# Block-diagonal B built on VectorE and stores issued in another order, in a four-layer kernel with two selective scans

## The chip, the cores and the metric

The kernel runs as one program on one core of a Trainium2 chip. The metric is the device time of one execution in microseconds (us), the median of several executions. A core has five engines with queues of their own: PE (TensorE, matrix products; its weight loads are listed as PEld), DVE (VectorE), ACT (ScalarE), POOL (GpSimd) and SP, which here only issues DMA transfers. Engines wait for each other and for transfers through counting semaphores that the program sets.

## The reference

Input x is 4 x 1024 x 512 in float32. Four layers follow each other: full attention with a softmax, attention that is linear in the sequence length, and two state-space layers ("layer 2" and "layer 3" here, as in the names of the code). Layer 3 works on a permutation of the rows. The core of a state-space layer is

```
xz = xn @ W_in ; x_in, z = split(xz)             # 1024 channels each
u = silu(causal_conv4(x_in) + conv_b)
dt_r, B, C = split(u @ W_xp)                     # 64, 16, 16 wide
dt = softplus(dt_r @ W_dt + b_dt)
h = h * exp(dt[t] * A) + (dt[t] * u[t]) * B[t]   # 1024 channels x 16 states, along 1024 steps
y[t] = sum over states of h * C[t]
out = x + gate * (((y + u * D) * silu(z)) @ W_out)
```

## The kernel before

The program is a row of stages, each a block that all engines enter together, with its own tiles in on-chip memory (SBUF and PSUM); results go from stage to stage through scratch tensors in device memory. The stages are `project` p0 (normalisation and the q, k, v products), `attention`, `project` p1 (output product of the first layer), `linear_layer`, then `ssm_inputs` and `scan` for layer 2 and again for layer 3, and a final gather.

**project** loops over the 4 batch elements. Rows of a batch element arrive in one of two x buffers (`Rows.load`, two transfers of 1024 KB), DVE takes their statistics (`take_stats`, L387) when it reaches output o = 0 of the element before, and centres them (L410) after o = 2; PE turns them around between later outputs. SP issues everything in one order: the rows of element it + 1 at the start of element it (from it = 1 on), for p1 the residual rows, and then the store of each output tile. p0 has 24 outputs to an element, p1 has 8.

**ssm_inputs** also loops over the 4 elements, with one x buffer. For each there is a part in which x_in, the convolution (L1660, L1664) and u are made in 8 blocks m, and a part in which z, dt and the product dt*u are made in 8 blocks. dt*u is then turned by PE (`turn`, L1473) into PSUM, copied as a high part by ACT (`copy_hi`, L1550) and as a low part by DVE (`take_lo`, L1642) into a tile dT, of which there are two, and stored (`store_dT`, two transfers of 512 KB). The turns of element it are made between the x products of element it + 1: `copy_hi(it, m)` writes the tile that block m - 2 used, so it waits for that store to land. `turn` of block m waits for the low part of block m - 1. DVE, between `take_lo` and `convolve`, also takes the statistics of the rows of the next element, one block for each m. SP stores blocks m = 0 to 7 of an element's dT during the next element, one ahead of each uD store. For the last element, blocks 0 to 3 are turned and stored between the dt blocks and blocks 4 to 7 after the last four z outputs (`z_end`).

**scan** takes half sequences of 512 steps in 16 blocks per element, each with 16 states. PE makes the input term ("drive") as a product of dT with a block-diagonal matrix of B, `Bd`, 128 x (16, 32, 16): on partition p only the entries with t = p mod 32 are nonzero. ACT copies the drive from PSUM into h (`lay`, L2078) and makes the decays exp(dt*A) (`decay`, L2102); DVE runs the recurrence (L2171), POOL multiplies by C (L1938), PE adds over states (L1972). There are two `Bd` tiles, for the first and the second half of a sequence. At the start of the stage DVE clears both (L2176), then SP and ACT each issue 16 transfers of 4 KB that put the diagonal of the first one in place (L1805, L2090). The second one and all later contents are loaded during the scan in 32 transfers each, onto the places that stay the same.

The lines that start the scan on ACT are

```
            for n in range(4):
                lay(n)
            for k in range(LOOP):
                if k < UNITS_ALL:
                    decay(k)
                if k + 4 < UNITS_ALL:
                    lay(k + 4)
```

Of the kernel before, what the change touches and what calls it, by code (L numbers as in the profile page):

```python
# [13 lines left out]
F32R = mybir.dt.float32r  # L14
# [438 lines left out]
def project(core, name, ident, eps, io, cols, src, tab, func, jobs, scr=None):  # L453
# [4 lines left out]
    with ExitStack() as ctx:  # L458
# [174 lines left out]
        def _(sp):  # L633
# [13 lines left out]
            for it in range(B):  # L647
                if it >= 1 and it + 1 < B:
                    rows.load(sp, it + 1)
                if has_res:  # L650
                    for k in range(8):
                        if it >= 1:
                            sp.wait_ge(staged[k].handle, staged[k].at(it * uses))
                        sp.dma_start(res[k][:], jobs[0]["residual"][it, k * P:(k + 1) * P, :]
                                     ).then_inc(core.slot_in[k].handle, 16)
                for o, (n, a, b) in enumerate(outs):
                    slot, u, job = o % 8, it * uses + o // 8, jobs[n]
                    sp.wait_ge(staged[slot].handle, staged[slot].at(u + 1))
                    if job["kind"] == "T" and split:
                        tile = parts[slot][:].rearrange("p (s t) -> p s t", s=2)  # L660
                        dst = job["dst"][it, :, a * P:(a + 1) * P, b * HALF:(b + 1) * HALF].rearrange("s p t -> p s t")
                    elif job["kind"] == "T":
                        tile, dst = stage[slot][:], job["dst"][it, :, a, b * HALF:(b + 1) * HALF]
                    else:
                        tile, dst = value_of(slot), job["dst"][it, b * P:(b + 1) * P, a * D:(a + 1) * D]
                    sp.dma_start(dst, tile).then_inc(stored[slot].handle, 16)
                    if beside is not None and 1 <= it <= 2 and o == 4:
                        beside.load(sp, it)
                    if beside is not None and it == 3 and o == 12:
                        beside.store(sp)  # L670
# [637 lines left out]
def ssm_inputs(core, ident, cols, eps, io, scr, layer, src, tab, gather=None):  # L1308
# [5 lines left out]
    with ExitStack() as ctx:  # L1314
# [55 lines left out]
        def _(sp):  # L1370
# [26 lines left out]
            for it in range(B):  # L1397
                if gather is None and it + 1 < B:
                    rows.load(sp, it + 1)
                for m in range(IB + 1):  # L1400
                    if it and m < IB:
                        store_dT(it - 1, m)
                    if m >= 1:
                        w(sp, "uD", it * IB + m)
                        sp.dma_start(scr["uD"][it, m - 1], uD[(m - 1) % 2][:]).then_inc(uD_out[(m - 1) % 2].handle, 16)
# [10 lines left out]
                for m in range(IB):  # L1416
                    zs = {0: [z_with(it, k) for k in range(4)], 2: z_mid(it), 4: [z_with(it, k) for k in range(4, 8)]}.get(m, ())
                    for n in zs:
                        store_z(it, 2 * IB + n)
                        if it == B - 1 and m == 4:  # L1420
                            store_dT(it, zs.index(n))
                    w(sp, "dt", it * IB + (m + 1))
                    sp.dma_start(scr["dt"][it, m], dt[m % 4][:]).then_inc(dt_out[m % 4].handle, 16)
            for n in z_end(B - 1):
                store_z(B - 1, 2 * IB + n)
            for m in range(4, IB):
                store_dT(B - 1, m)
            for k in range(2):
# [112 lines left out]
        def _(act):  # L1541
# [19 lines left out]
            for it in range(B):  # L1561
# [39 lines left out]
                for group in (range(0, 4), range(4, 8)):  # L1601
# [27 lines left out]
                    for m in group:  # L1629
                        nc.scalar.activation(ea[m % 4][:], ea[m % 4][:], ACT.Ln, bias=eps[:, 2:3]).then_inc(c["log"].handle, 1)  # L1630
                for n in z_end(it):
                    take_z(n)
            for m in range(4, IB):
                copy_hi(B - 1, m)

        @block.vector
        def _(dve):
# [31 lines left out]
            for it in range(B):  # L1669
# [51 lines left out]
                if it + 1 < B:  # L1721
                    take_lo(it, 1)
                finish_dt(6)
                finish_dt(7)
            for m in range(4, IB):
                take_lo(B - 1, m)

# [18 lines left out]
def scan(core, ident, zero_eps, io, scr, layer, residual, dst):  # L1746
# [7 lines left out]
    with ExitStack() as ctx:  # L1754
# [22 lines left out]
        s.update({"o_" + n: core.count("out_" + n) for n in ("turned", "copied", "made", "gated")})  # L1777
        s.update({"last_" + n: core.count("last_" + n) for n in ("turned", "copied")})
        crep_in = core.slot_in[0:4]
        bd_in, dt_in, dT_in = core.input_in[0:2], core.input_in[2:4], core.slot_in[4:6]  # L1780
# [20 lines left out]
        def _(sp):  # L1801
            def load_B(half, rows):
                b, th = half // 2, half % 2
                for t in rows:
                    sp.dma_start(Bd[th][t::TC, :, t, :],  # L1805
                                 scr["Bcol"][b, th, :, t].rearrange("j c (k n) -> j (c k) n", n=NS)).then_inc(bd_in[th].handle, 16)
# [65 lines left out]
            def store_o(n):  # L1872
                w(sp, "o_gated", n + 1)
                sp.dma_start(dst[n // TT, n % TT * P:(n % TT + 1) * P, :], o[:]).then_inc(o_out.handle, 16)

            sp.dma_start(A[:], scr["A"][layer - 2].rearrange("i p e -> p i e")).then_inc(s["A_in"].handle, 16)
            load_dt(0)
            load_dT(0)
            load_C(0, 0)
            w(sp, "cleared", 1)  # L1880
            load_B(0, range(0, TC, 2))
            for q in range(1, 4):
                load_C(0, q)
            load_dT(1)
            load_dt(1)
            w(sp, "cleared", 2)
            for blk in range(BLOCKS + IB + 2):
# [57 lines left out]
        def _(pe):  # L1945
            def make_drive(n):
# [5 lines left out]
                if n % 8 == 0:  # L1952
                    pe.wait_ge(dT_in[j].handle, dT_in[j].at(64 * (blk // 2 + 1)))
                    if m == 0:
                        pe.wait_ge(bd_in[th].handle, bd_in[th].at(16 * TC * (b + 1)))
                if n >= 1:
# [114 lines left out]
        def _(act):  # L2071
# [15 lines left out]

            w(act, "cleared", 1)
            for t in range(1, TC, 2):
                act.dma_start(Bd[0][t::TC, :, t, :],  # L2090
                              scr["Bcol"][0, 0, :, t].rearrange("j c (k n) -> j (c k) n", n=NS)).then_inc(bd_in[0].handle, 16)
            act.wait_ge(s["A_in"].handle, s["A_in"].at(16))
# [19 lines left out]
            def copy_late(step):  # L2112
# [6 lines left out]
                nc.scalar.copy(dst_, src_).then_inc(s["last_copied"].handle, 1)  # L2119

            for n in range(4):
                lay(n)
            for k in range(LOOP):
                if k < UNITS_ALL:
                    decay(k)
# [13 lines left out]
        def _(dve):  # L2139
# [61 lines left out]
    s["carried"].stage_added(UNITS_ALL // 8)  # L2201
    s["cleared"].stage_added(2)
    s["A_in"].stage_added(16)
    for k in range(2):
        bd_in[k].stage_added(16 * TC * B)
        dt_in[k].stage_added(16 * BLOCKS // 2)
# [152 lines left out]
```

## Time and profile before

| | us |
|---|---|
| median of 3 runs | 6346.13 (6344.94 to 6351.1) |
| the profiled execution | 6348.06 |
| its span, first to last instruction | 6346.3 |
| busy PE, DVE, ACT, POOL | 5510.1, 4684.1, 4206.4, 2482.3 |
| first instruction of scan 2, of scan 3 | 2922.56, 4947.09 |

The profile is one execution. Times of rows are microseconds from the start of the span, unless they are marked ns. A row of the timeline merges like instructions of one engine that follow each other: start, length of the stretch, engine, line, operation, output and inputs, how often; in brackets how long the engine had been idle before and who released it. SPq and ACTq rows are DMA issues; their length is the time of issuing. PEclk is the granted TensorE clock as a share of full speed.

### The profile page before, as it was taken

The page shows a single profiled execution, that of the slowest core. Times are in us where ns is not written, and L with a number is a line of the kernel's source. Part 1 is how long each engine was busy: PE and PEld are TensorE (multiplying, and loading weights), DVE is VectorE, ACT ScalarE, POOL GpSimd, SP SyncE. Part 2 cuts the span into 40 slices and gives each one's busy share as a digit, 9 for nine tenths or more (in the row PEclk, how much of TensorE's full clock was granted, in tenths as well). Part 3 has the DMA queues.
Part 4 walks back from the last instruction along what each step waited for, and adds up shares of the span by engine and source line. Part 5 has one row for each costly group of instructions (what it writes and reads, how often), then busy time and mean ns, then how long its engine had stood idle before and what let it go on. Part 6 is the DMA issues. An engine that isn't in the chain of part 4 may idle for free. (4 is left out here: it accounts for less than half of the span.)

```text
span 6346.3 us, 85966 instructions
## 1 busy us (share of the span) xinstructions
PE 5510.1 (87%) x30568; PEld 3517.3 (55%) x30568; DVE 4684.1 (74%) x5708; ACT 4206.4 (66%) x6218; POOL 2482.3 (39%) x1098
## 2 busy tenths in 40 slices
PE   8989999997899989995788888879999578888884
PEld 3456666664455534444666666654444466666662
DVE  3359999995545445546999999964555799999993
ACT  2148888883232235556989999954555799999981
POOL 0000000000000000003999999960000699999994
PEclk9999999998999999997999999999999899999997
DMA  6463333413211133336556566632444555665554
GB/s 232 183 150 68 87 78 81 101 35 144 102 44 50 34 115 147 148 135 190 151 153 162 161 162 160 158 110 90 148 150 155 171 152 160 156 159 156 158 144 175
DMA packets 571129, 842.72 MB, mean 133 GB/s; under 512 B 100544, under 2 KB 239936, under 8 KB 570704
## 3 DMA queue, kind: packets, MB, share of 16 engines
q1 hardware_dynamic: 559248, 811.92, 43.7%
q0 software_dynamic: 5120, 16.78, 0.8%
q10 hardware_dynamic: 6336, 8.52, 0.4%
q8 instruction: 246, 4.03, 0.3%
q14 instruction: 179, 1.47, 0.1%
HBM read 544.23 MB, written 292.81 MB: 132 GB/s over the span
## 5 line engine op out<-in xcount | busy, mean ns | idle before, releaser
L1938 POOL TENSOR_TENSOR scan_hC<-scan_h,scan_Crep 128x1024 f32<-128x1024 f32 x1024 | 2395.8, 2374 | 2413.8 <-DVE scan_h L2171 2392.9
L2102 ACT ACTIVATE scan_a<-scan_dt,scan_A 128x512 f32<-128x512 f32 x2048 | 1368.4, 697 | 91.0 <-DVE scan_h L2171 73.9
L1972 PE MATMUL scan_y<-ident,scan_hC 128*128 128x128 f32 x8192 | 1113.2, 279 | 293.9 <-POOL scan_hC L1938 288.3
L1972 PEld LDWEIGHTS scan_y<-ident,scan_hC 128*128 128x128 f32 x8192 | 903.8, 141 | 681.5 <-POOL scan_hC L1938 631.3
L2171 DVE TENSOR_TENSOR_SCAN scan_h<-scan_a,scan_carry,scan_h 128x512 f32<-128x512 f32 x1024 | 1216.6, 1258 | 17.0 <-ACT scan_a L2102 14.0
L2171 DVE TENSOR_TENSOR_SCAN scan_h<-scan_a,scan_h 128x512 f32<-128x512 f32 x1024 | 1155.0, 1198 | 59.3 <-ACT scan_a L2102 58.7
L2078 ACT COPY scan_h<-scan_drive 128x1024 f32<-128x1024 f32 x1024 | 1042.1, 1018 | 168.4 <-PE scan_drive L1960 156.4
L1960 PE MATMUL scan_drive<-scan_Bd,scan_dT 128*128 128x256 f32 x4096 | 750.3, 305 | 127.5 <-ACT scan_h L2078 76.5
L1960 PEld LDWEIGHTS scan_drive<-scan_Bd,scan_dT 128*128 128x128 f32 x4096 | 558.1, 192 | 180.6 <-issue 93.8
L861 DVE CUSTOM_DVE_ANT_0 att_sm<-att_S,att_mneg 128x1024 f32<-128x1024 f32 x512 | 621.8, 1215 | 16.5 <-POOL att_mneg L787 16.2
L919 ACT ACTIVATE att_pr<-att_sm,att_nmax 128x1024 f32<-128x1024 f32 x512 | 590.6, 1154 | 58.0 <-DVE att_nmax L861 45.5
L811 PE MATMUL att_TP<-ident,att_pr 128*128 128x128 f32 x4096 | 548.4, 277 | 12.6 <-ACT att_pT L904 12.6
L811 PEld LDWEIGHTS att_TP<-ident,att_pr 128*128 128x128 f32 x4096 | 457.3, 141 | 136.5 <-issue 52.0
L1492 PE MATMUL ssmin_ring<-ssmin_Wz,ssmin_xT 128*128 128x512 f32 x1024 | 462.1, 602 | 8.2 <-ACT ssmin_zt L1567 8.2
L1998 PE MATMUL scan_O<-scan_Wo,scan_gT 128*128 128x512 f32 x896 | 456.9, 593 | 0.0
L1492 PE MATMUL ssmin_ring<-ssmin_xT,ssmin_Wx 128*128 128x512 f32 x1024 | 454.6, 599 | 0.0
L869 DVE COPY att_pT<-att_TP 128x512 f32<-128x512 f32 x512 | 352.6, 689 | 100.1 <-PE att_TP L811 100.1
L787 POOL TENSOR_SCALAR att_mneg<-att_mrow 128x1024 f32<-128x1024 f32 x4 | 14.6, 3639 | 1011.4 <-DMA att_mrow<-mask 753.2
L800 PE MATMUL att_S<-att_k,att_q 128*128 128x512 f32 x1024 | 370.9, 444 | 18.7 <-DMA att_k<-scratch_k_split 11.5
L1684 DVE TENSOR_SCALAR ssmin_dt<-ssmin_DTP,column_tables 128x1024 f32<-128x1024 f32 x64 | 82.2, 1284 | 410.7 <-PE ssmin_DTP L1525 410.7
L904 ACT COPY att_pT<-att_TP 128x512 f32<-128x512 f32 x512 | 295.0, 576 | 105.4 <-PE att_TP L811 105.4
L1492 PEld LDWEIGHTS ssmin_ring<-ssmin_Wz,ssmin_xT 128*128 128x128 f32 x1024 | 190.4, 191 | 259.3 <-issue 236.7
(188 smaller groups left out, 6173.5 us busy)
## 6 DMA issues: line engine op xcount, KB each, us to landing
scan_dT<-scratch_dtuT SPq DMA_DIRECT2D x512, 256.0 KB, 6.1
scratch_dtuT<-ssmin_dT SPq DMA_DIRECT2D x128, 512.0 KB, 3.6
scan_Crep<-scratch_bc SPq DMA_DIRECT2D x64, 1024.0 KB, 9.5
att_q<-scratch_q_split SPq DMA_DIRECT2D x256, 128.0 KB, 4.5
att_k<-scratch_k_split SPq DMA_DIRECT2D x256, 128.0 KB, 4.7
scratch_uD<-ssmin_uD SPq DMA_DIRECT2D x64, 512.0 KB, 3.4
scratch_z<-ssmin_zt SPq DMA_DIRECT2D x128, 256.0 KB, 2.2
scratch_dt<-ssmin_dt SPq DMA_DIRECT2D x64, 512.0 KB, 2.6
```

Source lines behind the costliest of these rows:

```text
L800: last = nc.tensor.matmul(S[u % 2][:, half * HALF:(half + 1) * HALF], q[slot][:, t * P:(t + 1) * P].bitcast(F32R), k[slot][:, half * HALF: ...
L811: last = nc.tensor.transpose(TP[:, m * P:(m + 1) * P], pr[u % 2][:, m * P:(m + 1) * P], ident[:])
L861: nc.vector.tensor_tensor_reduce(sm[u % 2][:], S[u % 2][:], mneg[b % 2][:], -1.0, HUGE, ALU.add, ALU.min, nmax[u % 2][:]).then_inc(s["shif ...
L919: nc.scalar.activation(pr[u % 2][:], sm[u % 2][:], ACT.Exp, bias=nmax[u % 2][:, 0:1], scale=-1.0, accum_out=psums[:, u // PAIRS % 4, j, se ...
L1492: last = nc.tensor.matmul(ring[e % 4][:], lhs, rhs, start=(kt == 0), stop=(kt == KT - 1))
L1938: nc.gpsimd.tensor_tensor(hC[k % 2][:], of, Crep[:, 2 * p:2 * p + 2, :], ALU.mult).then_inc(s["scaled"].handle, 1)
L1960: last = nc.tensor.matmul(drive[:, c * TC:(c + 1) * TC, :], dT[j][:, at * P:(at + 1) * P].bitcast(F32R), Bd[th][:, at, :, first:first + GS ...
L1972: last = nc.tensor.matmul(y[j][:, t, :], hC[k % 2][:, i, t * P:(t + 1) * P], ident[:], start=(p == 0 and i == 0 and t == 0), stop=False, i ...
L1998: last = nc.tensor.matmul(O[:], gT[:, m, :], Wo[:, m, :], start=(m == 0), stop=(m == IB - 1))
L2078: nc.scalar.copy(h[group % 3][:, :, tt * P:(tt + 1) * P], drive[:].rearrange("p t n -> p n t")).then_inc(s["laid"].handle, 1)
L2102: nc.scalar.activation(a[(2 * k + i) % 3][:], dt[j][:], ACT.Exp, scale=A[:, m, 2 * p + i:2 * p + i + 1]).then_inc(s["decayed"].handle, 1)
L2171: nc.vector.tensor_tensor_scan(of, a[(2 * k + i) % 3][:], of, first, ALU.mult, ALU.add).then_inc(s["scanned"].handle, 1)
```

## The change

The first `Bd` of a scan is no longer cleared and filled by 32 small transfers. SP loads B as plain columns, 128 x 256 values, with one transfer (`raw`, in the tile o that is free then). DVE makes a mask (`diag`: 1 where t = p mod 32) by two small additions from the identity, and writes `Bd[0]` by 8 multiplications of 128 x 1024 (`spread`), each a quarter of the chunks and half of the states; PE's first 8 drives wait for one of them each. Then DVE clears `Bd[1]` as before. ACT issues no transfers and makes the first decays ahead of its first four copies. SP's three later C loads, dT(1) and dt(1) no longer wait for a cleared `Bd`.

In `ssm_inputs` the stores of dT blocks 0 and 1 move from the next element's first part to just ahead of the dt stores of blocks 4 and 6; the rows of element it + 2 (layer 2 only) are loaded ahead of the store of dt block 6 instead of at the start of element it + 1; and at the end of the last element the four z outputs, the four `copy_hi`, the four `take_lo` and their stores are interleaved. In `project` the rows of element it + 2 are loaded after the store of output o = 1 of element it.

```diff
-                if it >= 1 and it + 1 < B:
-                    rows.load(sp, it + 1)
...
                     sp.dma_start(dst, tile).then_inc(stored[slot].handle, 16)
+                    if o == 1 and it + 2 < B:
+                        rows.load(sp, it + 2)
...
-                if gather is None and it + 1 < B:
-                    rows.load(sp, it + 1)
+                if gather is None and it == 0:
+                    rows.load(sp, 1)
                 for m in range(IB + 1):
-                    if it and m < IB:
+                    if it and 2 <= m < IB:
                         store_dT(it - 1, m)
...
+                    if it + 1 < B and m in (4, 6):
+                        store_dT(it, m // 2 - 2)
+                    if gather is None and it + 2 < B and m == 6:
+                        rows.load(sp, it + 2)
+                    if it == B - 1 and m >= 6:
+                        store_z(it, 2 * IB + z_end(it)[m - 6])
+                        if m == 7:
+                            store_dT(it, 4)
                     w(sp, "dt", it * IB + (m + 1))
                     sp.dma_start(scr["dt"][it, m], dt[m % 4][:]).then_inc(dt_out[m % 4].handle, 16)
-            for n in z_end(B - 1):
-                store_z(B - 1, 2 * IB + n)
-            for m in range(4, IB):
-                store_dT(B - 1, m)
+            store_z(B - 1, 2 * IB + z_end(B - 1)[2])
+            store_dT(B - 1, 5)
+            store_z(B - 1, 2 * IB + z_end(B - 1)[3])
+            store_dT(B - 1, 6)
+            store_dT(B - 1, 7)
...
-                for n in z_end(it):
+                for n, m in zip(z_end(it), range(4, IB)):
                     take_z(n)
-            for m in range(4, IB):
-                copy_hi(B - 1, m)
+                    copy_hi(it, m)
...
                 finish_dt(5)
                 if it + 1 < B:
                     take_lo(it, 1)
+                else:
+                    take_lo(it, 4)
                 finish_dt(6)
+                if it == B - 1:
+                    take_lo(it, 5)
                 finish_dt(7)
-            for m in range(4, IB):
-                take_lo(B - 1, m)
+            take_lo(B - 1, 6)
+            take_lo(B - 1, 7)
...
+            sp.dma_start(raw, scr["Bcol"][0, 0].rearrange("j t c e -> (j t) (c e)")).then_inc(raw_in.handle, 16)
             sp.dma_start(A[:], scr["A"][layer - 2].rearrange("i p e -> p i e")).then_inc(s["A_in"].handle, 16)
             load_dt(0)
             load_dT(0)
             load_C(0, 0)
-            w(sp, "cleared", 1)
-            load_B(0, range(0, TC, 2))
             for q in range(1, 4):
                 load_C(0, q)
             load_dT(1)
             load_dt(1)
-            w(sp, "cleared", 2)
...
+                if n < SPREAD:
+                    w(pe, "cleared", n + 1)
...
-            w(act, "cleared", 1)
-            for t in range(1, TC, 2):
-                act.dma_start(Bd[0][t::TC, :, t, :],
-                              scr["Bcol"][0, 0, :, t].rearrange("j c (k n) -> j (c k) n", n=NS)).then_inc(bd_in[0].handle, 16)
...
+            decay(0)
             for n in range(4):
                 lay(n)
             for k in range(LOOP):
-                if k < UNITS_ALL:
+                if 1 <= k < UNITS_ALL:
                     decay(k)
...
-            for k in range(2):
-                zeros = zero_eps[:, 1:2].broadcast_to([P, NC * TC * NS])
-                nc.vector.tensor_copy(Bd[k][:].rearrange("p c t n -> p (c t n)").bitcast(F32R), zeros
-                                      ).then_inc(s["cleared"].handle, 1)
+            def spread(n):
+                tt, first = n % 4, n // 4 * GS
+                values = raw.rearrange("p (a o n) -> p a o n", o=1, n=NS)[:, tt::4, :, first:first + GS]
+                places = diag.rearrange("p (o t q) -> p o t q", o=1, q=1)
+                shape = [P, NC // 4, TC, GS]
+                nc.vector.tensor_tensor(Bd[0][:, tt::4, :, first:first + GS].bitcast(F32R), values.broadcast_to(shape),
+                                        places.broadcast_to(shape), ALU.mult).then_inc(s["cleared"].handle, 1)
...
+            for n in range(SPREAD):
+                spread(n)
+            zeros = zero_eps[:, 1:2].broadcast_to([P, NC * TC * NS])
+            nc.vector.tensor_copy(Bd[1][:].rearrange("p c t n -> p (c t n)").bitcast(F32R), zeros
+                                  ).then_inc(s["cleared"].handle, 1)
```

## Rows read from the trace of the kernel before

**Rows 1.** Scan 2: stretch, busy PE, PEld, DVE, ACT, POOL, clock, DMA, GB/s.

```profile
3000.00:3100.00 100.00, 69.39 (x537) 60.77 (x538) 99.76 (x93) 95.83 (x141) 100.00 (x44) 1.00 0.53 143
```

**Rows 2.** Timeline, the start of scan 2.

```profile
2922.56 0.36 SPq L1876 DMA_DIRECT2D scan_A<-scratch_A  x1
2922.59 8.76 DVE L2176 CAST scan_Bd<-eps 128x8192 fp32r<-128x8192 f32 x2 [4.66 <-PEq L1314]
...
2923.59 1.85 SPq L1822 DMA_DIRECT2D scan_dT<-scratch_dtuT  x4
...
2927.05 13.07 SPq L1805 DMA_DIRECT2D scan_Bd<-scratch_Bcol  x16
...
2941.58 1.20 PE L1960 MATMUL scan_drive<-scan_Bd,scan_dT 128*128 128x256 f32 x4 [24.99 <-DMA scan_Bd<-scratch_Bcol]
...
2950.88 1.28 ACT L2102 ACT_TABLE_LOAD   x1
...
2952.97 9.13 DVE L2171 TENSOR_TENSOR_SCAN scan_h<-scan_a,scan_h 128x512 f32<-128x512 f32 x8 [21.61 <-ACT scan_a L2102]
```

**Rows 3.** DMA rate in 40 slices of 0.35 us from 2923; issues, size, us to landing.

```profile
GB/s 0 12 107 98 140 293 304 345 228 211 199 170 217 228 217 199 258 199 199 187 199 205 164 228 228 322 386 374 393 383 211 72 34 35 31 30 20 24 20 14
...
scan_dt<-scratch_dt SPq DMA_DIRECT2D x1, 256.0 KB, 4.5
scan_A<-scratch_A SPq DMA_DIRECT2D x1, 68.0 KB, 2.2
```

**Rows 4.** Instructions by line and shape: count, busy us, mean ns, idle before.

```profile
L1693 DVE TENSOR_TENSOR ssmin_u<-ssmin_dt,ssmin_u 128x1024 f32<-128x1024 f32 x64 | 78.4, 1225 | 2.2
...
L1204 DVE TENSOR_TENSOR lin_q<-lin_q,lin_qmax 128x2048 f32<-128x2048 f32 x8 | 18.3, 2292 | 0.3
...
L1697 DVE TENSOR_TENSOR ssmin_BT<-ssmin_X,ssmin_BT 128x128 fp32r<-128x128 f32 x8 | 2.3, 292 | 10.7 <-ACT ssmin_BT L1619 10.7
```

**Rows 5.** Timeline, the end of layer 2's inputs; page, one line of the issues.

```profile
2903.82 4.67 SPq L1375 DMA_DIRECT2D scratch_z<-ssmin_zt  x4
2906.86 1.28 ACT L1567 ACTIVATE ssmin_zt<-ssmin_ring 128x512 f32<-128x512 f32 x2 [6.43 <-DMA scratch_z<-ssmin_zt]
...
2914.66 0.69 DVE L1642 TENSOR_TENSOR ssmin_dT<-ssmin_X,ssmin_dT 128x512 fp32r<-128x512 f32 x1 [0.16 <-ACT ssmin_dT L1550]
...
2917.24 0.69 DVE L1642 TENSOR_TENSOR ssmin_dT<-ssmin_X,ssmin_dT 128x512 fp32r<-128x512 f32 x1 [0.16 <-ACT ssmin_dT L1550]
...
scratch_dtuT<-ssmin_dT SPq DMA_DIRECT2D x128, 512.0 KB, 3.6
```

**Rows 6.** Timeline by engine, layer 2's inputs, from element 0 to 1.

```profile
2445.57 2.04 PE L1473 MATMUL ssmin_X<-ident,ssmin_u 128*128 128x128 f32 x8 [7.40 <-DVE ssmin_dT L1642]
...
2443.88 0.59 ACT L1550 CAST ssmin_dT<-ssmin_X 128x512 fp32r<-128x512 f32 x1 [12.82 <-DMA scratch_dtuT<-ssmin_dT]
...
2438.93 0.69 DVE L387 BATCH_NORM_STATS2 ssmin_st<-ssmin_x 128x6 f32<-128x512 f32 x1 [5.13 <-DMA ssmin_x<-scratch_x]
...
2444.76 0.67 DVE L1642 TENSOR_TENSOR ssmin_dT<-ssmin_X,ssmin_dT 128x512 fp32r<-128x512 f32 x1
...
2432.93 1.40 SPq L379 DMA_DIRECT2D ssmin_x<-scratch_x  x2
```

**Rows 7.** Timeline by engine, p1, from element 0 on.

```profile
1550.35 1.94 PE L420 MATMUL p_bank<-ident,p_x 128*128 128x128 f32 x8 [5.74 <-DVE p_x L410]
...
1565.62 17.33 PE L542 MATMUL p_bank<-p_W,p_xT 128*128 128x512 f32 x40
1588.61 1.94 PE L420 MATMUL p_bank<-ident,p_x 128*128 128x128 f32 x8 [5.66 <-DVE p_x L410]
...
1538.56 2.47 DVE L387 BATCH_NORM_STATS2 p_st<-p_x 128x6 f32<-128x512 f32 x4 [6.23 <-DMA p_x<-scratch_y]
```

**Rows 8.** Busy us by engine (columns as in rows 1), p0 from element 0 to 1.

```profile
120.00:140.00 20.00, 20.00 (x95) 7.58 (x94) 11.23 (x27) 5.62 (x8) 0.00 (x0) 1.00 0.44 160
```

**Rows 9.** Timeline, DVE's first recurrence of scan 3.

```profile
4978.11 9.13 DVE L2171 TENSOR_TENSOR_SCAN scan_h<-scan_a,scan_h 128x512 f32<-128x512 f32 x8 [22.22 <-ACT scan_a L2102]
```

More of the change, by code:

```diff
@@ L1778, in scan @@
         s.update({"last_" + n: core.count("last_" + n) for n in ("turned", "copied")})
+        raw_in = core.stage_stored[6]
+        raw, diag, pairs = o[:, 0:NC * NS], o[:, NC * NS:NC * NS + TC], o[:, NC * NS + TC:NC * NS + 3 * TC]
+        SPREAD = 8
         crep_in = core.slot_in[0:4]
@@ L1803, in load_B @@
                 b, th = half // 2, half % 2
+                if half == 1:
+                    w(sp, "cleared", SPREAD + 1)
                 for t in rows:
@@ L1953, in make_drive @@
                     pe.wait_ge(dT_in[j].handle, dT_in[j].at(64 * (blk // 2 + 1)))
-                    if m == 0:
-                        pe.wait_ge(bd_in[th].handle, bd_in[th].at(16 * TC * (b + 1)))
+                    if m == 0 and b + th >= 1:
+                        pe.wait_ge(bd_in[th].handle, bd_in[th].at(16 * TC * (b + th)))
+                if n < SPREAD:
+                    w(pe, "cleared", n + 1)
                 if n >= 1:
@@ L2172, in recur @@
                                                  ).then_inc(s["scanned"].handle, 1)
-            for k in range(2):
-                zeros = zero_eps[:, 1:2].broadcast_to([P, NC * TC * NS])
-                nc.vector.tensor_copy(Bd[k][:].rearrange("p c t n -> p (c t n)").bitcast(F32R), zeros
-                                      ).then_inc(s["cleared"].handle, 1)
+            def spread(n):
[5 more added lines that the diff above has]
+                                        places.broadcast_to(shape), ALU.mult).then_inc(s["cleared"].handle, 1)
+            nc.vector.tensor_tensor(pairs, ident[:, 0:2 * TC], ident[:, 2 * TC:4 * TC], ALU.add
+                                    ).then_inc(core.scalar_step.handle, 1)
+            dve.wait_ge(core.scalar_step.handle, core.scalar_step.at(1))
+            nc.vector.tensor_tensor(diag, pairs[:, 0:TC], pairs[:, TC:2 * TC], ALU.add
+                                    ).then_inc(core.scalar_step.handle, 1)
+            dve.wait_ge(core.scalar_step.handle, core.scalar_step.at(2))
+            dve.wait_ge(raw_in.handle, raw_in.at(16))
+            for n in range(SPREAD):
[3 more added lines that the diff above has]
+                                  ).then_inc(s["cleared"].handle, 1)
             for k in range(LOOP):
@@ L2201, in scan @@
     s["carried"].stage_added(UNITS_ALL // 8)
-    s["cleared"].stage_added(2)
+    s["cleared"].stage_added(SPREAD + 1)
+    core.scalar_step.stage_added(2)
+    raw_in.stage_added(16)
     s["A_in"].stage_added(16)
     for k in range(2):
-        bd_in[k].stage_added(16 * TC * B)
+        bd_in[k].stage_added(16 * TC * (B - 1 + k))
         dt_in[k].stage_added(16 * BLOCKS // 2)
```

## The prediction

> **What bounds the kernel now.** I read the page's slices first, then busy time by stage, then the timeline of each place that the diff touches, with the list of waits beside it to see which releaser comes last. No engine bounds the whole. In a scan it is DVE: in 100 us of scan 2 it is busy 99.76 [rows 1]. POOL and ACT are almost full there too, but their work follows DVE's. So a scan ends as much earlier as its first recurrence begins, as long as ACT and the dT loads keep up. In p0 PE never pauses, the border between two elements included [rows 8]. In p1 and in the first part of an element of `ssm_inputs` PE runs without a pause but for a hole at each border [rows 6, 7]. Thus three kinds of place can give something: the start of each scan, the end of each input stage (the next stage starts after it), and the holes at borders.
>
> **Start of a scan.** I count from T0, SP's first issue (2922.56). Now: DVE clears 2 x 4.4, the small transfers begin at T0+4.5 and hold PE until T0+19.0, four drives and lays take until T0+28.3, then a table load, the first decay, and the recurrence starts at T0+30.4 [rows 2]. In scan 3 DVE has idled 22.22 instead of 21.61, so it is T0+31.0 [rows 2, 9].
>
> After the change two paths run side by side.
>
> DVE: `raw` is 128 KB. The nearest rows are A, 68 KB in 2.2, and dt, 256 KB behind it, in 4.5 [rows 3]. It is first in the queue; I take 2.6, bounds 2.2 and 4.5. The two small additions end before that. The 8 spreads write 1024 elements each; a product of that size of two full operands takes 1.225, and one of 2048 with a repeated operand 2.292, so repeating costs nothing [rows 4]. Writing and reading in short runs: a low part of 128 elements in runs of 16 takes 0.292 [rows 4], which leaves no room for a large price per run, but runs of 8 with a repeated middle dimension are not in the trace. I take 1.15 from start to start (half of 2.292), 9.2 for eight; bounds 1.1 (the same rows less overlap) and 2.34 (128 elements in 0.292 scaled to 1024). The clear of `Bd[1]` adds 4.4. DVE is free at T0+2.6+9.2+4.4 = T0+16.2, bounds T0+15.4 and T0+27.6.
>
> The VectorE page speaks against a product here. The Trainium skill ("VectorE: DVE Perf Modes", "Why `tensor_tensor` can't do 2×_2P or 4×") has a float32 product of two tensors at one element per cycle where a copy makes two. The trace agrees: 1.20 ns an element against 0.53, the cleared `Bd` [rows 2, 4]. At the page's 0.96 GHz eight spreads would be 8.5, and DVE free 0.7 sooner, which by the next paragraph changes nothing.
>
> PE and ACT: the first drive now needs the first spread (T0+3.8) and dT(0). dT(0) is 4 x 256 KB, issued from T0+1.0 to T0+2.9 [rows 2]. From 2925.8 on the queues move about 210 GB/s, before the small transfers of B have begun [rows 3], so this is the rate of dT's own short rows; adding the slices, the 1.38 MB of A, dt and dT(0) are through at 2930.6, T0+8.0. `raw` ahead adds 0.4, and completion about 0.5. I take T0+8.8, bounds T0+7.0 (at the 345 of the best slice before) and T0+10.5. From the first drive to the end of the fourth lay it is 9.3 [rows 2]; the table load and the first decay lie in the wait before. The recurrence starts at T0+18.2: dT(0) decides, and the spreads have 2 us of slack. The second decay now stands behind lay 4 (a drive and lay take 2.3), where it was ready before; I take 0.5 for DVE's pause there. Gain: 30.4 - 18.2 - 0.5 = 11.7 in scan 2, 31.0 - 18.7 = 12.3 in scan 3, **24.0** in all; bounds for the two 6 (slow spreads: T0+27.6) and 29 (T0+16.2, where DVE decides).
>
> [...]
>
> SP is now free at once for 3 MB of C, dT(1) and dt(1). C's four parts and dT(1) follow dT(0): 4.2 MB at the 380 of the full slices, then 1.05 MB at 210, ends near T0+25.5; the ninth drive wants dT(1) near T0+27. Slack 1.5, so nothing; it is the first thing to be late.
>
> **End of an input stage.** Now z output 14 waits 6.43 for the store of z 12, which SP issues only behind four dt stores (2903.82), and all four copies of dT stand behind it; the last low part ends at 2917.93 [rows 5]. Afterwards `copy_hi(4)` runs at once behind z 12 (about 2900), and low part 4 is done at 2901.8. Blocks 5 to 7 each need `finish_dt` of the block (2.4) and the chain of turn, high and low part (2.58 from one block's last low part to the next's) [rows 4, 5]. Written out: low part 5 ends 2905.5, finish 7 ends 2907.9, low part 6 about 2909.4; `copy_hi(7)` needs the store of block 5, issued at 2907.5 behind dt 7 and z 14 and landing in 3.6 [rows 5], 2911.5, and the last low part ends about 2913.2. The 4.6 until the next stage stay. Gain 4.7 a stage, **9.4** for two; bounds 3 (store landing 5) and 6 (no store waited for) each.
>
> **p1.** DVE waits 6.23 for rows that SP loads only at the border, and PE 5.74 and 5.66 for the centred rows [rows 7]. An element's PE work is 64 products at 17.33/40 and 4 turns of some 0.9, 31.2, and the turns are 38.26 apart: 7.1 lost per border, pause and slower clock behind it together (the first turn after it takes 1.94) [rows 7]. Afterwards the rows are issued over 15 us before they are wanted. DVE then does statistics 5.6 earlier than PE's fourth product ends, output 2, and centres half in 1.9: PE waits perhaps 0.2. The second border's slow stretch looked a little longer, so I take 7.7 each, **15.4** for two; bounds 12 and 16.5.
>
> **Borders in layer 2's inputs.** ACT waits 12.82 for the store of dT(0), but that wait is not worth 12.82. Low part 2 starts at 2444.76, just when DVE is through with waiting for x (5.13, until 2438.93), statistics and a convolution; the high part was there about then as well [rows 6]. With dT(0) stored early, x alone decides. Its issue moves from 2432.93 to about 2429.6, but behind 1 MB of dT(1) where it had 0.5 MB of dt: +0.9. I take 2.4 for each of two borders, **4.8**; bounds 0 and 3.3 each. From element 2 to 3 and in layer 3 SP loads no x and DVE is the last already: 0.
>
> **p0.** PE is full [rows 8]; the moved loads give nothing. In element 0 SP now stands after o = 1 until the turn of the rows (a few us) and 2 MB go ahead of later stores; the slots come up for reuse 27 us after, so 0.
>
> **Sum.** 24.0 + 9.4 + 15.4 + 4.8 = 53.6. Against the profiled 6348.06 (span 6346.3) that gives 6294.5; the median is 1.9 below the profiled one, so **6292.5**. A measurement tells about 0.2%, 12.7 us.
>
> **Rivals.**
>
> *The spreads are slow* (short runs at 2.34 each): DVE decides at T0+27.6, no pause behind. Gain 2.8 + 3.4 = 6.2 in place of 24.0: 6310. For: the only row of such short runs; against: its fixed part. 0.10.
>
> *dT(0) or dT(1) is the late one*: 5.3 MB crowd one queue where 1.4 MB stood; if dT(1) is 3 us late or dT(0) comes at T0+10.5, each scan loses 2 to 3: 6298. 0.15.
>
> *The early rows give nothing in p1*, because centring or the residual loads then hold PE: 6292.5 + 15.4 = 6308. Against: DVE has 20 us of work in 31. 0.05.
>
> *dT(0) is early*: at the best slice's 345 GB/s it is there at T0+7.0, the fourth lay ends about when DVE is free (T0+16.2), DVE decides, and the scans give 2 x 2 more less a pause of DVE: 6288.5. Against: dT's own slices at 210. 0.10. [...]
>
> *Slower*: the spreads decide so strongly that the scans start later than now. Place: DVE, T0. With 29.6 gained elsewhere, each scan must start 14.8 later than T0+30.7, thus 8 spreads over 38.5, 4.8 each, four times the row. At 6.5 each (5.3 times) DVE is free at T0+59, 28.3 later than now per scan: 6346.1 - 29.6 + 56.6 = 6373. No row is near it. 0.02.
>
> *The change doesn't do what it says*, same within 0.2%: stores and loads land as late as before, and the scans lose to contention what they gain. 0.03.
>
> The forecast itself, 6284 to 6301, has 0.55. The range that leaves out no more than 2 in 10 is 6280 to 6310. Faster by over 0.2%: 0.95; within: 0.03; slower: 0.02.
>
> **What the profile of the changed kernel would show.** The first recurrence 18 to 19 after SP's first issue, released by ACT (decay or lay), with DVE idle some 2 before it; spreads near 1.15; PE's first drive released by the dT transfer. PE's holes in p1 gone and its clock 1.0 there. ACT without the 12.8 wait at layer 2's borders, but PE's 7.4 only down to about 5, with DVE still waiting for x. From the first instruction after the last dt group to scan's start 4.7 less. The prediction is wrong if spreads take over 1.4, if DVE pauses in the first 40 us of a scan for laid or dT, or if ACT waits over 3 for a dT store at an input stage's end.

## The result, and the profile after it

The changed kernel takes 6303.5 us (median of four, 6299.29 to 6306.85) where the kernel before takes 6348.2 beside it: a ratio of 0.9927 with a 95% interval of 0.9912 to 0.9942, by which the gain is 46 (37 to 56). Run again later it was at 0.9944 (0.9928 to 0.9960), a gain of 36 (25 to 46). The forecast was 6292.5 with a range of 6280 to 6310, a gain of 53.6. So the sign and the range held, the time is 11 above the forecast, and the gain is 7 to 18 below it. The profiled execution took 6299.29, span 6297.5: 48.8 less span than before.

Where the span went, from the same marks in both traces (an issue or a first instruction of each stage). Each stretch is one execution against one, and the scans differ between executions by more than 10, as is shown further below.

| mark | before | after | gain up to it | gain of the stretch | forecast |
|---|---|---|---|---|---|
| last copy of attention's output | 1464.8 | 1465.6 | -0.8 | -0.8 | 0 |
| first turn of the linear layer | 1655.95 | 1640.84 | 15.1 | p1: 15.9 | 15.4 |
| rows issued for layer 2's inputs | 2240.80 | 2225.39 | 15.4 | 0.3 | 0 |
| first issue of scan 2 | 2922.56 | 2900.97 | 21.6 | inputs: 6.2 | 9.5 |
| index load of layer 3's inputs | 4267.3 | 4230.8 | 36.5 | scan 2: 14.9 | 11.7 |
| first issue of scan 3 | 4947.09 | 4908.49 | 38.6 | inputs: 2.1 | 4.7 |
| index load of the gather | 6263.9 | 6214.5 | 49.4 | scan 3: 10.8 | 12.3 |
| end | 6346.3 | 6297.5 | 48.8 | -0.6 | 0 |

**Start of a scan** (beside [rows 2]): timeline of the kernel after, scan 2.

```profile
2900.97 0.33 SPq L1893 DMA_DIRECT2D scan_o<-scratch_Bcol  x1
...
2902.44 1.85 SPq L1839 DMA_DIRECT2D scan_dT<-scratch_dtuT  x4
...
2903.05 9.17 DVE L2194 TENSOR_TENSOR scan_Bd<-scan_o 128x1024 fp32r<-128x1024 f32 x8 [1.60 <-DMA scan_o<-scratch_Bcol]
2912.14 4.42 DVE L2207 CAST scan_Bd<-eps 128x8192 fp32r<-128x8192 f32 x1
...
2910.76 1.22 PE L1977 MATMUL scan_drive<-scan_Bd,scan_dT 128*128 128x256 f32 x4 [18.86 <-DMA scan_dT<-scratch_dtuT]
2913.18 1.19 PE L1977 MATMUL scan_drive<-scan_Bd,scan_dT 128*128 128x256 f32 x4 [1.19 <-ACT scan_h L2095]
...
2905.84 1.28 ACT L2115 ACT_TABLE_LOAD   x1 [11.07 <-DMA scan_dt<-scratch_dt]
2907.13 1.30 ACT L2115 ACTIVATE scan_a<-scan_dt,scan_A 128x512 f32<-128x512 f32 x2
...
2919.18 1.01 ACT L2095 COPY scan_h<-scan_drive 128x1024 f32<-128x1024 f32 x1 [1.38 <-PE scan_drive L1977]
...
2920.23 2.34 DVE L2185 TENSOR_TENSOR_SCAN scan_h<-scan_a,scan_h 128x512 f32<-128x512 f32 x2 [3.67 <-ACT scan_h L2095]
2923.28 7.11 DVE L2185 TENSOR_TENSOR_SCAN scan_h<-scan_a,scan_h 128x512 f32<-128x512 f32 x6 [0.71 <-ACT scan_a L2115]
```

T0 is SP's first issue of the scan, here 2900.97. The first drive comes at T0+9.8, released by dT(0); DVE is through with the spreads and the clear at T0+15.6, waits 3.67 for the fourth lay, and the recurrence starts at T0+19.3. The last row has the pause that follows, 0.71, behind the second decay. By the slices under the next heading the 1.51 MB of `raw`, A, dt(0) and dT(0) are through at about T0+8.2 (an estimate, adding them up), and the first drive begins 1.6 after that. In scan 3 the recurrence starts at 4927.45, T0+19.0.

**dT(1).** DMA rate of the kernel after in 40 slices of 0.875 from 2900.

```profile
GB/s 0 0 155 133 222 262 206 206 225 213 199 213 384 382 391 386 384 391 386 386 389 386 384 346 183 208 213 222 201 204 267 211 0 0 173 295 187 227 211 174
```

C runs at 380 to 390, then dT(1), dt(1) and uD at some 210 to 2928. The ninth drive, the first on dT(1), begins at 2930.07 with no wait in front of it. dT(1) has a slack of 2 at least.

**p1** (beside [rows 7]): timeline of the kernel after.

```profile
1545.16 1.06 PE L420 MATMUL p_bank<-ident,p_x 128*128 128x128 f32 x8
...
1576.32 1.06 PE L420 MATMUL p_bank<-ident,p_x 128*128 128x128 f32 x8
...
1590.15 31.07 PE L542 MATMUL p_bank<-p_W,p_xT 128*128 128x512 f32 x72
...
1532.81 4.84 DVE L387 BATCH_NORM_STATS2 p_st<-p_x 128x6 f32<-128x512 f32 x8
```

No pause stands before a turn, and the turns are 31.16 apart, where 38.26 was. DVE takes the statistics of all eight blocks at one go.

**Border in layer 2's inputs** (beside [rows 6]): timeline of the kernel after, element 0 to 1.

```profile
2413.98 0.97 SPq L1381 DMA_DIRECT2D scratch_dtuT<-ssmin_dT  x2
2414.99 2.17 SPq L379 DMA_DIRECT2D ssmin_x<-scratch_x  x2
...
2422.18 0.69 DVE L387 BATCH_NORM_STATS2 ssmin_st<-ssmin_x 128x6 f32<-128x512 f32 x1 [2.84 <-DMA ssmin_x<-scratch_x]
...
2428.83 1.94 PE L1482 MATMUL ssmin_X<-ident,ssmin_u 128*128 128x128 f32 x8 [5.12 <-DVE ssmin_dT L1650]
```

ACT's wait of 12.82 for a dT store is gone: none of the 50 copies of high parts from 2400 to 2850 waits for a store. PE's hole went from 7.40 to 5.12 only, and DVE still waits for x.

**End of layer 2's inputs** (beside [rows 5]): timeline of the kernel after, last element.

```profile
2883.53 0.43 SPq L1375 DMA_DIRECT2D scratch_z<-ssmin_zt  x1
2884.01 1.52 SPq L1381 DMA_DIRECT2D scratch_dtuT<-ssmin_dT  x2
2886.76 0.33 SPq L1431 DMA_DIRECT2D scratch_dt<-ssmin_dt  x1
2887.14 1.07 SPq L1375 DMA_DIRECT2D scratch_z<-ssmin_zt  x1
2888.26 1.97 SPq L1381 DMA_DIRECT2D scratch_dtuT<-ssmin_dT  x2
...
2888.03 0.58 ACT L1559 CAST ssmin_dT<-ssmin_X 128x512 fp32r<-128x512 f32 x1 [4.19 <-DMA scratch_dtuT<-ssmin_dT]
...
2892.75 0.59 ACT L1559 CAST ssmin_dT<-ssmin_X 128x512 fp32r<-128x512 f32 x1 [2.24 <-DMA scratch_dtuT<-ssmin_dT]
...
2894.80 0.69 DVE L1650 TENSOR_TENSOR ssmin_dT<-ssmin_X,ssmin_dT 128x512 fp32r<-128x512 f32 x1 [0.73 <-ACT ssmin_dT L1559]
2901.00 0.22 DVE L2197 TENSOR_TENSOR scan_o<-ident 128x64 f32<-128x64 f32 x1 [5.51 <-PEq L1314]
```

From `finish_dt(4)`, DVE's first step that completes dt of block 4 (2875.29; 2895.02 before), to the end of the last low part it is 20.2 now and was 22.9. But from there to the scan's first issue it is 5.5, and was 4.6: the end gave 1.9. In layer 3 the same marks give 20.2 and 5.4, also 1.9. What SP waits for last in the stage is the landing of the last dT store (waits of SP, kernel before and after, at the end of layer 2's inputs):

```profile
SPq L1432 <- DMA scratch_dtuT<-ssmin_dT: 3.4, 1, 3.4
SPq L1441 <- DMA scratch_dtuT<-ssmin_dT: 3.8, 1, 3.8
```

SP's last issue ends 0.4 after the last low part before (2918.32) and 0.8 after it now (2896.30); the scan's first issue comes 4.2 and 4.7 behind that.

### The profile page after: what moved, and what is told of

The parts are those of the page before. It is cut to its first block and busy times, and to the rows that moved or that the text cites. A ratio compares the mean times of both kernels' runs of the same rounds, so it can differ in the third digit from the quotient of the medians.

```text
span 6297.5 us, 85938 instructions
## 1 busy us (share of the span) xinstructions
PE 5498.4 (87%) x30568; PEld 3509.0 (56%) x30568; DVE 4694.3 (75%) x5726; ACT 4204.3 (67%) x6218; POOL 2483.5 (39%) x1098
```

## The experiments

### The parts one by one

Four kernels are the kernel before with one part of the diff each, word for word as in the diff above: `project` alone, `ssm_inputs` alone, `scan` alone, and `ssm_inputs` without what it changes at the last element's end.

> The kernel before with the change in `project` alone (rows of element it + 2 loaded after output o = 1). By the prediction p1 gives 15.4 (bounds 12 to 16.5) and p0 nothing, so a ratio of 0.9976 to the kernel before; by the changed kernel's profile p1 gave 15.9 and p0 with attention lost 0.7, which would be a ratio of 0.9976 too if that loss is the change's own and 0.9975 if not. If the rows gave nothing the ratio is 1.000. In the profile PE has no pause over 1 us ahead of its turns in p1, and DVE's statistics don't wait for rows.

> The kernel before with the whole change in `ssm_inputs` alone. By the prediction 14.2 (two borders 4.8, two stage ends 9.4), a ratio of 0.9978. By the changed kernel's profile 8.3 (borders 4.3, ends 1.9 and 2.1), a ratio of 0.9987. If the difference between the two is other work that slid, and not the ends, this run comes out at the first of them.

> The kernel before with the whole change in `scan` alone. By the prediction 24.0 (each scan starts 12 us earlier), a ratio of 0.9962. By the changed kernel's profile the starts gave 21.4 net of DVE's pauses, and scan 2 ran another 3.8 faster in its later part at a clock of 1.00 where it had been 0.97 to 0.98: if that is the execution's and not the change's, the ratio is 0.9966; if the change brings it, 0.9960. First recurrence at 19.3 after SP's first issue in scan 2.

> The kernel before with the change in `ssm_inputs` but for the last element's end, which stays as before: only dT blocks 0 and 1 are stored earlier and the rows are loaded earlier. By the prediction 4.8, a ratio of 0.9992; by the changed kernel's profile 4.3. The run before this one less this one is what the two stage ends give: 9.4 by the prediction, 4.0 by the profile.

| kernel | ratio (95% interval) | gain |
|---|---|---|
| `project` | 0.9976 (0.9967 to 0.9985) | 15 (10 to 21) |
| `ssm_inputs` | 0.9980 (0.9972 to 0.9989) | 13 (7 to 18) |
| `scan` | 0.9984 (0.9975 to 0.9993) | 10 (4 to 16) |
| `ssm_inputs`, borders only | 0.9994 (0.9984 to 1.0005) | 4 (-3 to 10) |

`project` agrees with the 15.4 forecast, with 5 either way, and so do the borders as far as they can be told. The two ends can't be told from the difference of the second row and the last (9, with over 8 either way), only from the traces: from `finish_dt(4)` to layer 2's scan it is 25.7 in the profile of `ssm_inputs` alone and 27.5 in the one without the ends, which is the 1.9 again. `scan` is the surprise: its profile has the first recurrence at T0+19.2 and T0+20.5, but the time fell by 10 (4 to 16), not by 21 to 24.

### The scan's part in its place

Two kernels on one chip: the changed kernel again, and the changed kernel with the old `scan`.

> The changed kernel once more, on one chip with the three others of this group. 46 below the kernel before (ratio 0.9927, as at first). The three parts measured one by one gave 15.2, 12.7 and 10.2, together 38 (0.9940). If the scan's part was mis-measured or falls away when it stands alone, this run stays near 0.9927; if 0.9927 was a lucky one, it comes out near 0.9940.

> The changed kernel with the scan of before: project and inputs are changed, the scan isn't. By the parts measured alone 27.9 below the kernel before (0.9956). What the run before this one has over it is the scan's part in its real place: 21 to 24 by the starts of the scans in the profile (19.3 in place of 30.4, less 0.9 of pauses, twice), 10 by the run with the scan's change alone. In the latter case the later part of the scans is longer, and the DVE idle time by stretches of 100 us must show where.

The changed kernel came out at 0.9944 (0.9928 to 0.9960), five runs of mean 6307.4. With the old scan it was 0.9961 (0.9947 to 0.9976), five runs of mean 6320.8. The scan's part is 13 here, with runs of 6297.8 to 6317.9 against 6311.6 to 6325.2. The profiles with the same start sequence say where the rest went (the two scans together; "rest" is from the first recurrence to the end of the stage, scan 2 and scan 3):

| kernel | starts at T0+ | rest | both scans |
|---|---|---|---|
| before | 30.4, 31.0 | 1314.3, 1285.8 | 2661.5 |
| `project` alone | 29.9, 30.5 | 1303.8, 1283.8 | 2648.0 |
| `ssm_inputs` alone | 29.7, 30.3 | 1313.7, 1285.1 | 2658.8 |
| borders alone | 30.6, 30.8 | 1310.0, 1285.6 | 2657.1 |
| after, old scan | 30.5, 30.2 | 1319.0, 1281.4 | 2661.1 |
| after | 19.3, 19.0 | 1310.6, 1287.1 | 2635.8 |
| `scan` alone | 19.2, 20.5 | 1322.1, 1289.1 | 2650.9 |
| after, again | 19.2, 20.2 | 1313.9, 1285.2 | 2638.3 |
| after, rows earlier (below) | 19.4, 19.4 | 1313.2, 1287.2 | 2639.2 |
| after, stores earlier (below) | 19.0, 19.4 | 1321.5, 1286.6 | 2646.5 |

The starts are 10.9 earlier a scan on average (mean 30.4 of 29.7 to 31.0, and 19.4 of 19.0 to 20.5), 21.9 for two. The whole scans are 15.2 shorter on average (2657.3 and 2642.1). The rest of scan 2 differs by 15 between the executions of the old scan and by 12 between those of the new one, as much as the part to be measured. One stretch of the kernel with `scan` alone shows what such a difference is made of: busy us by engine, columns as in [rows 1].

```profile
3272.00:3277.00 5.00, 3.04 (x23) 2.21 (x21) 5.00 (x5) 3.73 (x7) 3.29 (x2) 1.00 1.04 334
3277.00:3282.00 5.00, 2.24 (x18) 1.83 (x16) 3.87 (x5) 4.14 (x6) 2.73 (x2) 1.00 1.06 242
3282.00:3287.00 5.00, 3.96 (x19) 3.96 (x20) 3.34 (x4) 1.34 (x4) 5.00 (x3) 0.53 0.71 161
3287.00:3292.00 5.00, 4.72 (x33) 4.48 (x31) 2.34 (x2) 3.46 (x7) 4.05 (x3) 0.79 0.59 170
3292.00:3297.00 5.00, 3.41 (x26) 2.72 (x25) 4.99 (x5) 5.00 (x8) 3.81 (x3) 1.00 1.00 250
```

PE is busy 5.3 of 10 us (3272 to 3282). Then the granted clock falls to 0.53 in a stretch of 5 us and is 0.79 in the next. DVE is busy 5.7 of these last 10 us where it is full otherwise. From 3276 to 3294 it waits 4.5 for decays, which stand in ACT's queue behind lays, and ACT waits 7.2 for PE's drives. The pause of PE that comes before has a source in the same trace, POOL's wait for a load of C:

```profile
3273.71 4.66 POOL L1941 TENSOR_TENSOR scan_hC<-scan_h,scan_Crep 128x1024 f32<-128x1024 f32 x2 [2.04 <-DMA scan_Crep<-scratch_bc]
3280.64 6.97 POOL L1941 TENSOR_TENSOR scan_hC<-scan_h,scan_Crep 128x1024 f32<-128x1024 f32 x3 [2.27 <-DMA scan_Crep<-scratch_bc]
```

PE then waits 1.96, 0.75 and 3.05 for POOL's products. In scan 2 POOL waits 3.4 to 15.4 for C in the fourteen profiles of this document. The four with over 10.5 are the four with the longest rest, 1319.0 to 1322.1; the ten others have 1303.8 to 1314.3. That ties the rest of scan 2 to the loads of C, but no run changed these loads, so that they cause the difference is not shown.

Stretches of 100 us with a clock under 1.00, beyond the first, number two to six in scan 2 and none to three in scan 3 of the ten profiles. In the mean over these profiles 6.7 are missing between 21.9 and 15.2. DVE idles 1.1 in the first 100 us of a scan where it idled 0.5, mostly the pause behind the second decay: 1.3 for two scans. In the eleven stretches of 100 us behind it it idles 31.5 in both scans where it idled 27.5, above all in those with a clock under 1.00: 4.0. The last 1.4 I can't place.

Whether the new scan itself brings more of this is not settled for scan 2. For scan 3 the table leans to yes, and the four other kernels with the new scan, described below, more so: their rest of scan 3 is 1290.8 (spreads twice), 1293.5 (dT(0) first), 1296.2 and 1289.6 (the two kernels of all together). Of nine executions with the new scan eight are above the longest of the five with the old one (1285.8). Some 0.6 a scan of this is the pause behind the second decay. What in the new scan brings the rest is open.

### Who decides the start

Three kernels change one thing in the changed one. The first makes every spread twice:

```diff
             for n in range(SPREAD):
-                spread(n)
+                for again in range(2):
+                    spread(n, again)
```

> The changed kernel with each of the 8 spreads made twice (the first one waited for, then the same again). It measures how much slack the spreads have. The prediction's theory is that dT(0) decides and DVE has slack: the profile after shows DVE free 15.6 after SP's first issue and the fourth lay's end at 19.2, a slack of 3.6. Eight more spreads are 9.2 to 10, so DVE is free at about 25 to 25.6, the first recurrence comes at about 25.5 in place of 19.3, and DVE's later pauses of 0.9 go: 5 to 5.5 a scan, 10 to 11 in all over the changed kernel (ratio to the kernel before 0.9943). If DVE decided, each scan would lose the full 9.2 to 10, 18 to 20 in all (0.9957).

The sixteen spreads took 19.25, DVE was free at T0+25.8, and the recurrences started at T0+25.7 and T0+25.6, with DVE idle before neither. So 10.1 more on DVE moved the start by 6.4: DVE had 3.7 of slack, as the wait for the fourth lay in the profile after says, and dT(0) with its four drives and lays decides. By time it was 0.9954 (0.9940 to 0.9968), 17 more than the first run of the changed kernel and 6 more than the second, around the 11 expected.

The second issues dT(0) earlier:

```diff
-            sp.dma_start(A[:], ...)
-            load_dt(0)
             load_dT(0)
+            sp.dma_start(A[:], ...)
+            load_dt(0)
```

> The changed kernel with the four transfers of dT(0) issued ahead of those of A and dt(0), right behind raw. If dT(0) decides, its 324 KB less in front bring it 1 us to 1.5 us earlier, and the first drive, the fourth lay and the first recurrence with it, as DVE is free 3.6 before: 2 to 3 in all over both scans (ratio 0.9923). dt(0) and A then land near 11.5, the first decay comes ahead of the first lay and holds it up by up to 1.5, which could eat the gain. If DVE decides, nothing.

Timeline of this kernel, scan 2 (T0 is 2903.99).

```profile
2911.78 1.22 PE L1977 MATMUL scan_drive<-scan_Bd,scan_dT 128*128 128x256 f32 x4 [16.82 <-DMA scan_dT<-scratch_dtuT]
...
2912.91 1.28 ACT L2115 ACT_TABLE_LOAD   x1 [15.10 <-DMA scan_dt<-scratch_dt]
2914.20 1.30 ACT L2115 ACTIVATE scan_a<-scan_dt,scan_A 128x512 f32<-128x512 f32 x2
...
2915.44 1.00 ACT L2095 COPY scan_h<-scan_drive 128x1024 f32<-128x1024 f32 x1
```

The first drive comes at T0+7.8, 2.0 earlier, and nothing is gained: the recurrence starts at T0+19.7. ACT's queue now has the first decay waiting for dt(0) in front of lay 0, and lay 0 comes at T0+11.4, where it came at T0+11.1. That is the wait behind a moved instruction that I had named as a risk. The time was 0.9933 (0.9916 to 0.9949), no difference from the changed kernel that can be told.

### Borders and ends

> The changed kernel with the rows of element it + 2 in layer 2's inputs loaded ahead of the store of dt block 5, not of block 6 behind the store of dT(1). By the prediction x alone decides at the border: DVE's wait of 2.84 for it goes, and PE's hole falls from 5.12 to about 2.3: 2.8 for each of two borders, 5.6 in all (ratio 0.9918). The rival is that ACT's wait for the store of dT(0) comes back, as that store now stands behind 1 MB: then less than 2 in all.

```diff
-                    if gather is None and it + 2 < B and m == 6:
+                    if gather is None and it + 2 < B and m == 5:
                         rows.load(sp, it + 2)
```

(the line also stands ahead of `store_dT` now). DVE's wait for x is gone, ACT waits for no dT store, and PE's hole is down to 2.18:

```profile
2430.58 1.71 PE L1482 MATMUL ssmin_X<-ident,ssmin_u 128*128 128x128 f32 x8 [2.18 <-DVE ssmin_dT L1650]
```

From the load of the first weight to the scan's load of A it is 665.8 where the changed kernel has 674.4 and 674.2. That is 8.5, more than the 5.6 expected; x did decide. The two holes account for 6.3 of it (5.12 and 5.54 fell to 2.18 each); the rest I did not follow up. The time was 0.9927 (0.9910 to 0.9943), which can't show it.

> The changed kernel with the stores of dT blocks 4 and 5 of the last element ahead of the dt stores of blocks 6 and 7. In the profile after, the store of block 4 is issued 2.0 after its low part is done, and ACT's high part 6 waits 4.19 for it; block 5's store is issued 2.6 after, and high part 7 waits 2.24. If the place in SP's order is what lost the ends, high part 7 and all behind it come 2 to 2.6 earlier in each of the two layers: 4 to 5 in all (ratio 0.9920). If the landing time decides and SP's order doesn't, under 1 in all.

```diff
                     if it == B - 1 and m >= 6:
                         store_z(it, 2 * IB + z_end(it)[m - 6])
-                        if m == 7:
-                            store_dT(it, 4)
+                        store_dT(it, m - 2)
...
-            store_dT(B - 1, 5)
```

Timeline of this kernel.

```profile
2885.87 0.58 ACT L1557 CAST ssmin_dT<-ssmin_X 128x512 fp32r<-128x512 f32 x1 [2.43 <-PE ssmin_X L1480]
...
2890.05 4.15 SPq L1381 DMA_DIRECT2D scratch_dtuT<-ssmin_dT  x4
...
2890.93 0.69 DVE L1648 TENSOR_TENSOR ssmin_dT<-ssmin_X,ssmin_dT 128x512 fp32r<-128x512 f32 x1 [0.16 <-ACT ssmin_dT L1557]
2898.91 0.23 DVE L2195 TENSOR_TENSOR scan_o<-ident 128x64 f32<-128x64 f32 x1 [7.29 <-PEq L1314]
```

No high part waits for a store any more, and from `finish_dt(4)` to the last low part it is 16.7, 3.5 less. But the stage's end then stands 7.3 behind the last low part, not 5.5. Half of what the chain gains is given back. The place is SP's queue: its stores now stand close together, the last four issues take 4.15, and the last of them ends 2.6 behind the last low part, where it was 0.8. From that issue to the scan's first it is 4.7, as in the changed kernel. The net is 1.7 in each layer by the traces, against the 2 to 2.6 expected. By time it was 0.9935 (0.9919 to 0.9952), no difference that can be told.

### All of it together

> The changed kernel with three things together: rows loaded ahead of dt block 5's store at layer 2's borders, dT blocks 4 and 5 stored ahead of dt 6 and 7 at the inputs' ends, and in the scan dT(0) issued behind raw, ahead of A and dt, with the first decay split around the first lays (lay 0, half, lay 1, half, lay 2, lay 3), so that it doesn't stand ahead of lay 0. Borders 2.9 each, 5.8; ends about 1.6 for layer 2 and 1 for layer 3; scans: first drive at T0+7.8, fourth lay done at about T0+17.7, first recurrence at T0+17.8 in place of 19.3, 1.5 each. 11 less than the changed kernel. If DVE decided the start instead, the scans give nothing and it is 8.

> The run before this one, and PE makes 32 transposes of the identity into the unused output bank at the start of each scan, while it waits for dT(0). In the profile after, the first drives take 1.19 at the lower clock (0.71 at the higher) with a period of 2.39, drive and lay in turn. If the transposes bring the granted clock up by the first drive, four drives are 4 x 0.48 shorter and the fourth lay is done at about T0+15.8, just behind DVE's end at T0+15.7: 1.9 less in each scan, 3.8 in all. If the clock doesn't rise in time, nothing.

The first has the three edits above and this one on ACT:

```diff
-            decay(0)
             for n in range(4):
                 lay(n)
+                if n < 2:
+                    decay(0, [n])
```

It ran at 0.9916 (0.9901 to 0.9931), mean 6290.8 beside 6307.4 of the changed kernel on the same chip: 16.6 less where 11 was expected, and it beats both kernels. The recurrences started at T0+17.8 and T0+18.2, as expected. The scans' share does not show: against the profile of the changed kernel run again, layer 2's inputs are 12.1 shorter and layer 3's 2.0, but the two scans together 4.7 longer, for all their earlier starts (2643.1; the rest is 1310.9 and 1296.2). The second adds 32 transposes by PE while it waits. It ran at 0.9917 (0.9903 to 0.9930), mean 6291.1: nothing gained. Its busy us by engine, from the scan's start, and two rows of its timeline:

```profile
2888.20:2893.20 5.00, 5.00 (x32) 4.77 (x31) 3.43 (x5) 0.00 (x0) 0.00 (x0) 0.71 0.86 199
2893.20:2898.20 5.00, 0.73 (x5) 0.54 (x4) 5.00 (x6) 0.78 (x1) 0.00 (x0) 0.98 1.10 280
2898.20:2903.20 5.00, 2.39 (x8) 1.86 (x8) 5.00 (x2) 4.19 (x6) 0.00 (x0) 0.50 1.04 387
```

```profile
2896.61 0.71 PE L1976 MATMUL scan_drive<-scan_Bd,scan_dT 128*128 128x256 f32 x4 [3.40 <-issue]
...
2898.57 1.19 PE L1976 MATMUL scan_drive<-scan_Bd,scan_dT 128*128 128x256 f32 x4 [1.25 <-ACT scan_h L2100]
```

The transposes did raise the clock, and the first drive took 0.71. Then PE waited, the clock fell back to 0.50, and the next drives took 1.19 again. The first drive also came later, at T0+8.6 where it was T0+7.7 without the transposes, and the recurrences started at T0+18.2 and T0+18.6.

## Why the prediction was right, and where it was not

- **Scan starts.** Right in mechanism: two paths, dT(0) decides, DVE has slack. I had the first drive at T0+8.8 and the recurrence at T0+18.2; it was T0+9.8 and T0+19.3 (19.0 in scan 3). The bytes were through as early as I had them (about T0+8.2), but from there to the first drive it was 1.6, where I had put 0.5 for completion. The spreads took 1.15 each from start to start, as taken. The pause was 0.9, not 0.5. The starts gave 23.2 in the profiled pair and 21.9 on average, not 25.0.
- **From start to end of the scan.** The step that failed is "a scan ends as much earlier as its first recurrence begins". The scans' term of 24.0 came to 10 (4 to 16) and 13 in time and to 15 in the mean over profiles. The rest of a scan differs between executions by as much as the gain, with the clock's dips in it, and I had no term for that. The two profiles of the first comparison happened to have the scans 25.7 apart (14.9 and 10.8). That looks like the forecast, and it is partly luck: against the ten profiles the old scan's rest was 2 long there in scan 2 and the new one's 6 short.
- **Ends of the input stages.** The term of 9.4 is mis-sized: the trace has 3.7. Two sub-steps failed. I let `copy_hi(7)` wait for a store and overlooked that `copy_hi(6)` waits in the same way for block 4's, which SP issues 2.0 after its low part, behind the stores of dt 6 and a z. That made the chain 2.0 longer than written (20.2, not 18.2), and ACT's wait of 4.19 there is over the 3 that I had named as a sign of being wrong. And "the 4.6 until the next stage stay" did not hold: 5.5, and 7.3 when the stores were moved further ahead. The stage end waits for the last store to land. The closer the stores stand together in SP's queue, the later its last issue ends behind the last low part: 0.4, 0.8 and 2.6.
- **p1.** 15.4 forecast, 15.9 in the trace, 15 (10 to 21) alone. The rows are as said. p0 and attention together were 0.8 longer in the profiled pair, where I had 0.
- **Borders of layer 2.** 4.8 forecast. From the rows' issue to `finish_dt(4)` of the last element it is 654.2 before and 649.9 after, 4.3. The three profiles with the old borders have 653.3 to 654.3, the eight with the new ones 647.7 to 652.3. That ACT's 12.8 was not worth 12.8 and that x decides held: moving x alone took it to 641.3.
- **Rivals.** Slow spreads, dT(1) late, dT(0) early and p1 without gain are all refuted by rows. dT(0) "late" (T0+10.5) is a little nearer to the T0+9.8 that happened than the forecast's T0+8.8.
- **The sum.** With what the runs gave for each term, 15 for p1, about 4 to 6 for the borders, 3.7 for the ends and 15 for the scans, it comes to 38 to 40, not 53.6. The range held in the first comparison with a gain of 46; the second gave 36, and 36 below the 6346.1 that the forecast started from is 6310, the edge of the range.

## What to carry to other kernels

When a wait is taken out of a chain, write down who is the next to be waited for on each buffer, block by block. The one that I left out cost 2 us a stage. What these stages' ends wait for is the landing of their last store. When the chain in front of the stores was shortened and they stood closer together in one queue, their last issue ended later behind the chain, and the stage got 1.9 of 2.7 the first time and 1.7 of 3.5 the second. And a start that comes earlier is worth its length only if the long part behind it is steady. Measure how much that part differs between executions of one program before a term is put on it.

## What the runs showed of the hardware

The granted TensorE clock falls in the middle of a scan, from 1.00 to about 0.5 (2.4 to 1.2 GHz) for some 5 us, after PE has run with pauses (5.3 busy of 10 in the rows above). How often differs between executions of the same program, and a stretch of 100 us with a dip has some 1 to 4 us more of DVE idle. Thirty-two transposes raised the clock from its lower level ahead of a scan, but PE then made one drive in 5 us, and the clock was back at the lower level for the next. The product with two repeated operands in runs of 8 elements costs what a plain one does: 1.22 for 1024 elements a partition (1.15 from start to start), beside 1.225. One SP issue of a dT store took 0.36 at the least and 1.23 at the most at the end of layer 2's inputs in the changed kernel.
